# Wide self-attention: the half-swapped copy of the values comes from ScalarE instead of TensorE

## The reference

```python
x = x + attn(layernorm(x))          # attn, for x of shape (B, N, D) = (128, 64, 128):
q = (x @ Wq).reshape(B, N, 16, 64).transpose(0, 2, 1, 3) * scale
k, v = split(x @ Wkv)               # 64 columns each, shared by all heads
sim = einsum('bhid,bjd->bhij', q, k) + relative position bias
sim = causal mask of sim
out = einsum('bhij,bjd->bhid', softmax(sim), v)
return merge_heads(out) @ Wout + bout
```

## Time and profile before

| | |
|---|---|
| time before, median of 3 runs | 2633.96 us (2633.53 to 2636.45) |
| the profiled execution: its own time | 2635.68 us |
| the profiled execution: its span, first to last instruction | 2633.9 us |
| busy share of the span: PE, PEld, DVE, ACT, POOL | 88%, 71%, 75%, 59%, 42% |
| mean granted TensorE clock, share of full speed | 0.949 |
| the phase of the change: first and last L542 | 48.2 us, 540.9 us |

### The profile page before, as it was taken

The page is one execution under the profiler, slowest core; times in us unless marked ns, Lnnn a source line. Parts: engine busy times, 40 slices in busy tenths (PEclk is TensorE's granted clock), DMA queues, the critical chain, the costliest instruction groups (busy, mean ns, idle before and its releaser), DMA issues. The chain is left out here.

```text
span 2633.9 us, 87347 instructions
## 1 busy us (share of the span) xinstructions
PE 2325.9 (88%) x31791; PEld 1879.2 (71%) x31791; DVE 1966.1 (75%) x5597; ACT 1551.2 (59%) x4181; POOL 1108.2 (42%) x1038
## 2 busy tenths in 40 slices
PE   7999999979999992424999979998999999999985
PEld 7888888856666662213888868887788888888863
DVE  3777777758888887897888857775777777777755
ACT  1666666548888882534888858886344444444432
POOL 0333333324444443003999969996222222222222
PEclk9999999989999996755999989999999999999998
DMA  4000000000000000001000000000000000000002
GB/s 114 2 0 0 0 0 0 0 8 15 15 15 15 15 15 1 0 0 33 1 0 0 0 1 1 0 0 4 8 7 6 6 6 6 6 6 6 6 2 64
DMA packets 56447, 25.43 MB, mean 10 GB/s; under 512 B 17635, under 2 KB 55846, under 8 KB 56358
## 3 DMA queue, kind: packets, MB, share of 16 engines
q1 hardware_dynamic: 52802, 23.06, 3.2%
q10 hardware_dynamic: 3556, 1.19, 0.2%
HBM read 20.04 MB, written 4.19 MB: 9 GB/s over the span
## 5 line engine op out<-in xcount | busy, mean ns | idle before, releaser
L706 POOL TENSOR_TENSOR sa_sc<-sa_sc,sa_rs 128x1024 f32<-128x1024 f32 x64 | 121.8, 1904 | 335.8 <-DVE sa_rs L682 335.8
L1762 POOL TENSOR_TENSOR lo_qk_r<-lo_qk_ms,w_neg_half 128x20 f32<-128x20 f32 x64 | 226.9, 3545 | 22.1 <-DVE lo_qk_ms L1685 22.1
L1762 POOL TENSOR_TENSOR gl_qk_r<-gl_qk_ms,w_neg_half 128x20 f32<-128x20 f32 x64 | 226.7, 3543 | 1.1 <-DVE gl_qk_ms L1685 1.1
L948 POOL TENSOR_TENSOR xa_sc<-xa_sc,xa_rs 128x1024 f32<-128x1024 f32 x64 | 121.7, 1902 | 157.7 <-DVE xa_rs L924 157.7
L485 POOL TENSOR_TENSOR xan_ve<-xan_mv,w_eps_ln 128x1 f32<-128x1 f32 x64 | 13.4, 209 | 393.6 <-DVE xan_mv L479 393.6
L852 ACT ACTIVATE xan_xT<-xa_misc 128x128 f32<-128x128 f32 x64 | 17.7, 277 | 269.6 <-PE xa_misc L764 269.6
L785 PEld LDWEIGHTS xa_qs<-xan_xT,late_x_wq 128*128 128x128 f32 x1024 | 119.1, 191 | 52.7 <-issue 52.7
L921 DVE TENSOR_REDUCE xa_sm<-xa_sc 128x16 f32<-128x1024 f32 x64 | 78.1, 1220 | 89.1 <-ACT xa_sc L864 89.1
L679 DVE TENSOR_REDUCE sa_sm<-sa_sc 128x16 f32<-128x1024 f32 x64 | 78.1, 1221 | 80.4 <-ACT sa_sc L637 80.4
L1184 POOL TENSOR_TENSOR ca_kz<-ca_kt,w_constant 128x512 f32<-128x512 f32 x128 | 130.9, 1043 | 15.3 <-ACT ca_kt L1118 15.3
L561 PE MATMUL sa_qs<-san_xT,w_a_wq 128*128 128x128 f32 x1024 | 132.3, 283 | 1.7 <-DVE sa_sc L668 1.7
(11 more groups left out here) (331 smaller groups left out, 7014.5 us busy)
## 6 DMA issues: line engine op xcount, KB each, us to landing
w_x<-in_x_dram SPq DMA_DIRECT2D x8, 512.0 KB, 7.2
ca_cx<-in_ctx_dram SPq DMA_DIRECT2D x64, 64.0 KB, 1.8
xa_cx<-in_ctx_dram SPq DMA_DIRECT2D x64, 64.0 KB, 1.7
out_dram<-la_out SPq DMA_DIRECT2D x16, 256.0 KB, 2.3
ca_mask<-in_mask_BxSxS_ff_dram SPq DMA_DIRECT2D x64, 32.0 KB, 1.7
w_a_wq<-in_L_attn_Wq_dram SPq DMA_DIRECT2D x1, 512.0 KB
w_a_wo<-in_L_attn_Wout_dram SPq DMA_DIRECT2D x1, 512.0 KB
prep_xwo<-in_L_xattn_Wo_dram ACTq DMA_DIRECT2D x1, 512.0 KB
```

Source lines behind the costliest of these rows:

```text
L706: pool.tensor_tensor(v, v, bcast(rs[:, s, :], 2, S), ALU.mult).then_inc(prob_done, 1)
L948: pool.tensor_tensor(v, v, bcast(rs[:, s, :], 2, S), ALU.mult).then_inc(prob_done, 1)
L1762: pool.tensor_tensor(qk_r[:, s, :], qk_ms[:, s, :], k["neg_half"][:, 0:NQK], ALU.pow).then_inc(sg["qk_r"], 1)
```

## The change

PE no longer computes the second order of the values. The two products of L551 are gone, and the semaphore of the group is now raised by the product of L549. ACT's one copy of both planes (L625, 128 x 128) becomes three copies of 64 columns: all 128 rows into plane 0, rows 64 to 127 of PSUM into rows 0 to 63 of plane 1, and rows 0 to 63 into rows 64 to 127. Each raises `v_done`, so the two waits on it count three for a tile.

```diff
@@ turn, PE
-                    after(pe, v_done, t, 1)
+                    after(pe, v_done, t, 1, per=3)
@@ key_value, PE
-                    pe.matmul(misc[:, 2 * P:2 * P + DH], xT[:, s, :], k["a_wv"][:, :], start=True, stop=True)
-                    for r in range(2):
-                        last = pe.matmul(misc[r * 64:r * 64 + 64, 2 * P + DH:3 * P], xT[:, s, (1 - r) * 64:(2 - r) * 64],
-                                         k["a_wv"][:, :], start=True, stop=True)
-                    last.then_inc(kv_psum, 1)
+                    pe.matmul(misc[:, 2 * P:2 * P + DH], xT[:, s, :], k["a_wv"][:, :], start=True, stop=True).then_inc(kv_psum, 1)
@@ attend, PE
-                    after(pe, v_done, t)
+                    after(pe, v_done, t, per=3)
@@ key_value, ACT
-                    act.activation(vx[:, four, :, :].rearrange("p a d -> p (a d)"), misc[:, 2 * P:3 * P], ACT.Copy).then_inc(v_done, 1)
+                    act.activation(vx[:, four, 0, :], misc[:, 2 * P:2 * P + DH], ACT.Copy).then_inc(v_done, 1)
+                    for r in range(2):
+                        act.activation(vx[r * 64:r * 64 + 64, four, 1, :], misc[64 - r * 64:128 - r * 64, 2 * P:2 * P + DH],
+                                       ACT.Copy).then_inc(v_done, 1)
```

## The result

The changed kernel takes 2708.35 us, median of 4 runs (2703.84 to 2709.06), against 2633.78 for the kernel before (median of 4, 2633.53 to 2636.45): a ratio of 1.0277, with a 95% interval of 1.0259 to 1.0295. It is 75 us slower; 26 us faster was forecast.

What follows compares the result with a forecast made beforehand. PE's own instruction stream, without idle time, was taken as the bound; 60 steady steps x 0.42 = 25.2 plus 0.8 for the fill gave 26.0 us, so 2634.0 - 26.0 = 2608.0 us, range 2605 to 2619.

Steps and rivals of the forecast that it cites:

- the sum's silent assumption: Whole kernel: 26.0 us gained in the first phase, taken off 2634.0 for 2608.0, with no change reckoned for other phases.
- The one on the slower side: Rival, first phase: ACT's three value copies become the pace-setter, up to 2657 us; chance 0.04.
- The stalls at the change of tile: PE around L551, first phase: both stalls go with the two products, saving 0.42 us a step, 0.15 of it ahead of L551.
- the one on drains (Key Properties): PE at L551: a change of tiling mode drains the array, so both stalls go, saving 0.42 us a step.
- the one on speed-up (Theoretical Speedup): PE at L551: two column tiles side by side cost as little as one product, saving only 0.22 us a step.
- the stalls stay: Rival, PE around L551: a step gains only 0.27 or 0.22 us, giving 2617 or 2620 us; chance 0.13.
- The price of the copies: ACT, first phase: the three value copies take 0.25 us each, hidden in ACT's waits, so they cost nothing.
- T + 4.39: ACT, first phase: when the three value copies end their turn, counted from T, the start of a step's scores.
- The cover of 0.24 us between DVE's read and PE's queries: First phase: time PE's queries have to spare after DVE's read of the scores; ACT's lateness beyond 0.24 us is lost.
- The fill of the pipeline: First four steps of the first phase: 0.8 us gained (two times 0.42), as the queries already wait for DVE.

Runs made afterwards that it cites:

- e3: The kernel before with only ACT's part of the change, three 64-column copies, PE still computing the second order: 2637.29 us, ratio 1.0004.
- e5: The changed kernel plus 91 idle semaphore increments on PE ahead of the barrier between the feed-forward's halves: 2611.39 us, ratio 0.9909 to the kernel before.
- e13: The changed kernel plus 14 idle increments on PE ahead of the feed-forward's barrier, loop at place 43: 2707.23 us in a single run.
- e1: The changed kernel plus 91 idle semaphore increments on PE just before the feed-forward's down product: 2621.65 us, ratio 0.9943 to the kernel before.
- e2: The kernel before, self-attention untouched, plus 165 idle semaphore increments on PE just before the feed-forward's down product: 2746.35 us, ratio 1.0412.
- e10: The changed kernel plus 209 idle increments on PE ahead of the feed-forward's barrier, loop at place 238: 2616.31 us in a single run.
- e15: The changed kernel plus 227 idle increments on PE ahead of the feed-forward's barrier, loop at place 0: 2646.36 us in a single run.

## Why the prediction was wrong

**The step that failed is the sum's silent assumption** that what isn't edited keeps its time. "2634.0 - 26.0" charges the change with the first phase alone. The shift of PE's program put the cross-attention's loop on a place where it touches 8 blocks. It then fetches 9 at a jump (8 and presumably the next) and loses 90 us / 13 = 6.9 us each time. Some 4.5 of the 6.9 are the two waits (58.6 us / 13), and the rest is mostly the lower clock after them (0.50 to 0.55 from 2042 to 2048 us, 1.00 before and behind). There was a sign: this loop has 194 matmul records a tile, the first phase's 125, with four tiles a pass in both. By the Trainium skill, "Runtime: NRT & Kernel Launch", Instruction fetch mechanics, PE holds 2048 instructions, of which 1599 is four fifths. I had counted neither bodies nor packets. None of my rivals had this place. The one on the slower side was ACT's copies, and e3 shows that they cost nothing.

**The stalls at the change of tile**: right, at 0.22 from load to load and 7.46 us a step where 7.45 was forecast. Of the two rules of the Trainium skill, "TensorEngine Tiling (Array Packing)", the one on drains (Key Properties) gave the right sum here, 0.41 us a step, and the one on speed-up (Theoretical Speedup) the wrong one, 0.22. The rival "the stalls stay" is out.

**The price of the copies**: right, 0.25 each. The first query copy starts at 307.64 = T + 4.39 as forecast, and ACT catches up by the second.

**The cover of 0.24 us between DVE's read and PE's queries**: sized from a step without a jump of DVE. One step in four has DVE's pause of 0.33, and there DVE reads the scores late and PE waits (0.18 us ahead of L557):

```profile
312.44 1.29 DVE L667 SCALAR_TENSOR_TENSOR sa_sc<-sa_qs,w_a_bias 128x512 f32<-128x512 f32 x2
```
```profile
313.78 1.86 PEld L557 LDWEIGHTS sa_qs<-san_xT,w_a_wq 128*128 128x128 f32 x16 [0.18 <-DVE sa_sc L667]
```

That is 12 x 0.25 = 3 us of the 8 that are missing in the first phase. The pauses stood in the waits of the kernel before, hidden by its longer step:

```profile
DVE w_x L688 <- issue: 3.7, 11, 0.4
```

**The fill of the pipeline**: forecast at 0.8 us gained, measured 2.6 us lost in the profiled execution, as TensorE stayed at 1.2 GHz longer (clock 0.56 from 56 to 62 us; before, 1.00 from 54 us on). The change doesn't force that: in e5 the same code reached 1.00 by 54 us, its first four steps gained 0.6 us, and its first phase took 471.3 us, 21.4 less than before. Of the fifteen profiled executions with the changed first phase ten had the high clock from 54 to 60 us and five, that of the change's own run among them, the low one; all three with PE's old first phase had 0.93 or more. Whether the change makes the late clock likelier stays open. Over all of them the changed phase takes 471.3 to 474.8 us, the old one 492.7 to 494.7. Most of the rest is the step, 0.41 and not 0.42 gained, 59 times.

With the loop back in place, as in e5, the forecast of 2608.0 stands beside a measured 2611.39; single runs at other fast places took 2614.12 to 2618.81.

## What to carry to other kernels

Before judging an edit by its own stage, compare the packets on the instruction queue of the two pages: a jump from 55 to 172 says that a loop is being fetched again, wherever it is. The time of a PE loop of 1538 to 1792 instructions, which may touch 7 blocks or 8, can depend on where it starts, and so on every instruction ahead of it (seen here at 1599, worked out for the rest). Keep such a body at 1536 or fewer, or pad ahead of it in a pause, as e5 does, and look whether the pause has grown. And size a cover in the worst step of a pass, the one with the jump, not in the typical one.

## What the runs showed of the hardware that I had not expected

- PE's loop of 1599 instructions runs without any refetch where it touches 7 blocks of 256, and fetches 9 blocks of 16 KB at every jump, with PE idle for 4.3 to 4.9 us in the changed kernel and up to 5.3 in e13, where it lies squarely across 8 (places 24 to 43). The 2048 instructions that the Trainium skill, "Runtime: NRT & Kernel Launch", Instruction fetch mechanics, gives PE would be 8 blocks, and a loop across 8 should then fit. That a fetch ahead of the ninth block displaces the first would account for both, and for 9 packets a jump; it wasn't tested.
- At such a jump PE stops twice, first at the loop's first instruction and then at the block border behind it, which lies at the same place of the program in seven kernels (42 or 43 by the count of records).
- At the lower end of the slow places only some jumps are slow, 7 and 3 of 13. A race between the jump and the fetch ahead would look like this. It stays open, as does why there are fewer at place 0 than at 242.
- A semaphore increment on PE that does no work costs 0.15 us in a row of them: 74 more lengthen the wait ahead of the down product from 43.50 us (e1) to 55.05 (e2), and 18 more from 35.37 (e10) to 38.15 (e15). The 0.13 of the expectations came from how late the down product was, and part of the row is hidden in the pause.
- DVE's jump back costs 0.33 us with 4 tiles a pass and 0.46 to 0.51 with 8. Why it is longer there stays open.
